# Expert products with two 64-column stationary halves in the main tiles, and one eviction per main tile

## What is computed

```
all_h   = einsum('bsd,ndr->bsnr', x, neurons)          # f_know: 128 matrices of 192 x 128
h       = einsum('bsnr,bsn->bsr', all_h, weights)      # only 4 weights per token are not zero
all_out = einsum('bsr,nrd->bsnd', h, neurons)          # r_know: 128 matrices of 128 x 192
out     = einsum('bsnd,bsn->bsd', all_out, weights)    # only 4 weights per token are not zero
```

## Time and profile before

| | us |
|---|---|
| median of 3 runs | 1011.28 |
| lowest and highest run | 1009.06 and 1013.69 |
| span of the profiled execution | 1005.3 |

### The profile page before, as it was taken

How to read it: one execution, slowest core, us unless ns; L and a number is a source line. 1 busy time by engine, 2 the same in 40 slices (tenths; PEclk the granted TensorE clock), 3 DMA queues, 4 the chain that set the end, 5 groups by cost and what they waited for, 6 DMA issues and landing times.

```text
span 1005.3 us, 21117 instructions
## 1 busy us (share of the span) xinstructions
PE 842.1 (84%) x5575; PEld 692.3 (69%) x5575; DVE 691.8 (69%) x4357; ACT 431.6 (43%) x1339; POOL 552.8 (55%) x764
## 2 busy tenths in 40 slices
PE   5789999999999999977731799999999799699900
PEld 3778888888888777754420688999988458565800
DVE  2199999999999899947694599874444244255423
ACT  0134334434444344425430254444544488578800
POOL 5256556665666565525477471007773677673065
PEclk9689989989999599967555799999999799899955
DMA  9233443443433265201732876557898677588533
GB/s 319 96 136 125 171 170 136 148 145 140 169 115 118 103 205 184 89 21 34 183 104 75 260 244 174 140 154 204 283 408 335 210 261 254 191 276 283 191 106 90
DMA packets 81580, 177.17 MB, mean 176 GB/s; under 512 B 12952, under 2 KB 38232, under 8 KB 78648
## 3 DMA queue, kind: packets, MB, share of 16 engines
q1 hardware_dynamic: 56088, 120.62, 37.2%
q10 hardware_dynamic: 14112, 32.12, 8.3%
q0 software_dynamic: 11264, 23.09, 7.7%
HBM read 94.25 MB, written 81.53 MB: 175 GB/s over the span
## 4 chain that ended last, share of the span: by engine, by line
PE 31%; DVE 28%; POOL 17%; issue 13%; ACT 6%; DMA 3%; SPq 1%; ACTq 1%; POOLq 0%; DVEq 0%
PE bank L1198 17%; DVE work L1335 12%; DVE top L1329 9%; ACT m_y L926 5%; POOL early L742 5%; PE bank L1186 4%; POOL slots_g L749 3%; POOL slots_x L720 3%; PE bank L1243 2%; PE bank L954 1%; PE bank L974 1%; POOL eqbd L622 1%; PE bank L999 1%; DMA early<-in_vocab,ids 1%; POOL sc L672 1%
## 5 line engine op out<-in xcount | busy, mean ns | idle before, releaser
L1335 DVE MATCH_REPLACE8 work<-top,work 128x68 f32<-128x68 f32 x896 | 179.2, 211 | 0.1
L906 ACT ACTIVATE m_y<-bank 64x128 f32<-64x128 f32 x392 | 106.3, 271 | 144.9 <-PE bank L1198 142.6
L926 ACT ACTIVATE m_y<-bank 64x192 f32<-64x192 f32 x392 | 127.1, 324 | 49.7 <-PE bank L1243 27.0
L1198 PE MATMUL bank<-f_all,place 96*128 (+1 forms) x792 | 146.3, 329 | 0.0
L1329 DVE MAX8 top<-work 128x8 f32<-128x68 f32 x896 | 128.9, 213 | 6.5 <-ACT tru L792 6.2
L1198 PEld LDWEIGHTS bank<-f_all,place 96*128 96x128 f32 x792 | 117.4, 193 | 7.4 <-issue 0.2
L1243 PE MATMUL bank<-r_all,place 128*128 (+1 forms) x396 | 118.2, 423 | 0.2 <-ACT m_y L926 0.2
L742 POOL DMA_INDIRECT early<-slots_h,s_all x68 | 65.6, 964 | 89.2 <-DMA slots_h<-m_y 68.8
L1604 DVE COPY place<-bank 96x256 f32<-96x256 f32 x147 | 57.4, 417 | 81.5 <-PE bank L1186 77.1
L1612 DVE COPY place<-bank 128x128 f32<-128x128 f32 x147 | 38.0, 287 | 100.8 <-PE bank L1234 100.6
L954 PE MATMUL bank<-early,xp 128*128 128x192 f32 x432 | 94.2, 382 | 6.7 <-DMA xp<-in_a_x 5.2
(11 more groups left out here) (187 smaller groups left out, 1692.9 us busy)
## 6 DMA issues: line engine op xcount, KB each, us to landing
early<-slots_x SPq DMA_DIRECT2D x49, 384.0 KB, 3.9
slots_y<-m_y ACTq DMA_DIRECT2D x49, 384.0 KB, 3.2
slots_h<-m_y ACTq DMA_DIRECT2D x49, 256.0 KB, 4.4
early<-slots_g SPq DMA_DIRECT2D x49, 256.0 KB, 3.3
f_all<-in_f_know SPq DMA_DIRECT2D x16, 768.0 KB, 9.3
r_all<-in_r_know SPq DMA_DIRECT2D x16, 768.0 KB
slots_x<-zero SPq DMA_DIRECT2D x28, 360.0 KB, 3.0
slots_x<-zero SPq DMA_DIRECT2D x28, 336.0 KB, 3.3
```

Source lines behind the costliest of these rows:

```text
L906: last = nc.scalar.activation(m_yh[rows, d, t, :], bank[2 + t][rows, h * R:(h + 1) * R], ACT.Copy)
L926: last = nc.scalar.activation(m_y[rows, d, t, :], bank[2 + t][rows, h * D:(h + 1) * D], ACT.Copy)
L1198: last = nc.tensor.matmul(into, m_xT[t][0:HALF, c, :], matrix[:, ..., c * R:(c + 1) * R], start=(c == 0), stop=(c == 1))
L1335: last = nc.vector.match_replace(work[:, par, c, :], top8[:, c, :], work[:, par, c, :], TAKEN)
```

## The change

In main tiles each expert's 64 token columns become a stationary operand of their own. Half `h` multiplies only its own matrix and writes its own 64 partitions of the bank, at the same columns for both halves. The order is: for each feature half `c`, expert 0 and then expert 1. A main tile of the first product is then eight passes of 128 columns in place of four of 256, and of the second four passes of 192 in place of two of 384. ACT evicts a main tile with one instruction over 128 partitions in place of two over 64. Spill tiles, transposes, copies, loads, stores and all semaphores stay as they are.

```diff
--- before.py
+++ after.py
@@ -901,9 +901,12 @@
                     act.wait_ge(sem[f"m_out{d}"], 16 * (j // DEPTH))
                 for t in range(GROUP):
                     act.wait_ge(sem["m_mm0"], j * GROUP + t + 1)
-                    for h in range(2):
-                        rows = slice(h * HALVED, (h + 1) * HALVED)
-                        last = nc.scalar.activation(m_yh[rows, d, t, :], bank[2 + t][rows, h * R:(h + 1) * R], ACT.Copy)
+                    if first_order(g)[n] < PART_MAIN:
+                        last = nc.scalar.activation(m_yh[:, d, t, :], bank[2 + t][:, 0:R], ACT.Copy)
+                    else:
+                        for h in range(2):
+                            rows = slice(h * HALVED, (h + 1) * HALVED)
+                            last = nc.scalar.activation(m_yh[rows, d, t, :], bank[2 + t][rows, h * R:(h + 1) * R], ACT.Copy)
                     last.then_inc(sem["m_done0"], 1)
                 act.wait_ge(sem["m_done0"], (j + 1) * GROUP)
                 at = first_order(g)[n] * GROUP * P
@@ -921,9 +924,12 @@
                     act.wait_ge(sem[f"m_out{d}"], 16 * (in_turn(d, GROUPS) + j // DEPTH))
                 for t in range(GROUP):
                     act.wait_ge(sem["m_mm1"], j * GROUP + t + 1)
-                    for h in range(2):
-                        rows = slice(h * HALVED, (h + 1) * HALVED)
-                        last = nc.scalar.activation(m_y[rows, d, t, :], bank[2 + t][rows, h * D:(h + 1) * D], ACT.Copy)
+                    if j - FIRST_GROUP[g] < PART_MAIN:
+                        last = nc.scalar.activation(m_y[:, d, t, :], bank[2 + t][:, 0:D], ACT.Copy)
+                    else:
+                        for h in range(2):
+                            rows = slice(h * HALVED, (h + 1) * HALVED)
+                            last = nc.scalar.activation(m_y[rows, d, t, :], bank[2 + t][rows, h * D:(h + 1) * D], ACT.Copy)
                     last.then_inc(sem["m_done1"], 1)
                 act.wait_ge(sem["m_done1"], (j + 1) * GROUP)
                 act.dma_start(slots_y[g][(j - FIRST_GROUP[g]) * GROUP * P:(j - FIRST_GROUP[g] + 1) * GROUP * P, :].rearrange("(p t) d -> p t d", p=P),
@@ -1186,19 +1192,25 @@
                     last = nc.tensor.transpose(turn_bank[t][0:HALF, c * P:(c + 1) * P], m_x[:, d, t, c:D:2], ident[:])
                 last.then_inc(sem["m_turn0"], 1)
 
-            def multiply_first(j, t, pair):
+            def multiply_first(j, t, pair, fixed):
 
                 pe.wait_ge(sem["m_xt0"], j * GROUP + t + 1)
                 if j >= 1:
                     pe.wait_ge(sem["m_done0"], (j - 1) * GROUP + t + 1)
-                n = R * (2 // len(pair))
-                for h, matrix in enumerate(pair):
-                    into = bank[2 + t][:, h * n:(h + 1) * n]
+                if fixed:
                     for c in range(2):
-                        last = nc.tensor.matmul(into, m_xT[t][0:HALF, c, :], matrix[:, ..., c * R:(c + 1) * R], start=(c == 0), stop=(c == 1))
+                        for h, matrix in enumerate(pair):
+                            rows = slice(h * HALVED, (h + 1) * HALVED)
+                            last = nc.tensor.matmul(bank[2 + t][rows, 0:R], m_xT[t][0:HALF, c, rows], matrix[:, c * R:(c + 1) * R],
+                                                    start=(c == 0), stop=(c == 1))
+                else:
+                    for h, matrix in enumerate(pair):
+                        for c in range(2):
+                            last = nc.tensor.matmul(bank[2 + t][:, h * R:(h + 1) * R], m_xT[t][0:HALF, c, :], matrix[:, c * R:(c + 1) * R],
+                                                    start=(c == 0), stop=(c == 1))
                 last.then_inc(sem["m_mm0"], 1)
 
-            def first_product(g, n, pairs):
+            def first_product(g, n, pairs, fixed):
                 j = FIRST_GROUP[g] + n
                 for t in range(0, GROUP, AHEAD):
                     for ahead in range(t + AHEAD, t + 2 * AHEAD):
@@ -1207,7 +1219,7 @@
                         elif n + 1 < PART_GROUPS[g]:
                             turn_first(j + 1, ahead - GROUP)
                     for now in range(t, t + AHEAD):
-                        multiply_first(j, now, pairs[now])
+                        multiply_first(j, now, pairs[now], fixed)
 
             pe.wait_ge(sem["tiles_known"], 1)
             pe.wait_ge(sem["f_in0"], 16 * LATE)
@@ -1219,11 +1231,11 @@
                         pe.wait_ge(sem["f_in1"], 16 * (CHUNKS - LATE))
                     if jj < PART_MAIN:
                         at = [(jj * GROUP + t) * 2 for t in range(GROUP)]
-                        pairs = [[f_all[0:HALF, e:e + 2, :]] for e in at]
+                        pairs = [[f_all[0:HALF, e + h, :] for h in range(2)] for e in at]
                     else:
                         e = matrix_numbers(mybir.EngineType.PE, 2 * g, jj)
                         pairs = [[f_all[0:HALF, bass.ds(e[2 * t + h], 1), :].squeeze(1) for h in range(2)] for t in range(GROUP)]
-                    first_product(g, n, pairs)
+                    first_product(g, n, pairs, jj < PART_MAIN)
 
             def turn_second(j, t):
                 d = j % DEPTH
@@ -1233,17 +1245,20 @@
                     pe.wait_ge(sem["m_xt1"], (j - 1) * GROUP + t + 1)
                 nc.tensor.transpose(turn_bank[t][:, 0:P], m_h[:, d, t, :], ident[:]).then_inc(sem["m_turn1"], 1)
 
-            def multiply_second(j, t, pair):
+            def multiply_second(j, t, pair, fixed):
 
                 pe.wait_ge(sem["m_xt1"], j * GROUP + t + 1)
                 if j >= 1:
                     pe.wait_ge(sem["m_done1"], (j - 1) * GROUP + t + 1)
-                n = D * (2 // len(pair))
                 for h, matrix in enumerate(pair):
-                    last = nc.tensor.matmul(bank[2 + t][:, h * n:(h + 1) * n], m_xT[t][:, 0, :], matrix, start=True, stop=True)
+                    rows = slice(h * HALVED, (h + 1) * HALVED)
+                    if fixed:
+                        last = nc.tensor.matmul(bank[2 + t][rows, 0:D], m_xT[t][:, 0, rows], matrix, start=True, stop=True)
+                    else:
+                        last = nc.tensor.matmul(bank[2 + t][:, h * D:(h + 1) * D], m_xT[t][:, 0, :], matrix, start=True, stop=True)
                 last.then_inc(sem["m_mm1"], 1)
 
-            def second_product(g, j, pairs):
+            def second_product(g, j, pairs, fixed):
                 stop = FIRST_GROUP[g] + PART_GROUPS[g]
                 for t in range(0, GROUP, AHEAD):
                     for ahead in range(t + AHEAD, t + 2 * AHEAD):
@@ -1252,7 +1267,7 @@
                         elif j + 1 < stop:
                             turn_second(j + 1, ahead - GROUP)
                     for now in range(t, t + AHEAD):
-                        multiply_second(j, now, pairs[now])
+                        multiply_second(j, now, pairs[now], fixed)
 
             pe.wait_ge(sem["m_done0"], GROUPS * GROUP)
             pe.wait_ge(sem["r_in"], 16 * (NE // CHUNK))
@@ -1262,11 +1277,11 @@
                 for jj in range(PART_GROUPS[g]):
                     if jj < PART_MAIN:
                         at = [(jj * GROUP + t) * 2 for t in range(GROUP)]
-                        pairs = [[r_all[:, e:e + 2, :].rearrange("p e d -> p (e d)")] for e in at]
+                        pairs = [[r_all[:, e + h, :] for h in range(2)] for e in at]
                     else:
                         e = matrix_numbers(mybir.EngineType.PE, 2 * g + 1, jj)
                         pairs = [[r_all[:, bass.ds(e[2 * t + h], 1), :].squeeze(1) for h in range(2)] for t in range(GROUP)]
-                    second_product(g, FIRST_GROUP[g] + jj, pairs)
+                    second_product(g, FIRST_GROUP[g] + jj, pairs, jj < PART_MAIN)
 
 
         @block.vector
```

## The result

The changed kernel takes **987.61 us** in the median against 1010.17 for the kernel before in the same job. One of its four runs took 2220.68 us, for a reason that is not known, and the ratio leaves it out. The ratio of the means is 0.9768, 95% interval 0.9738 to 0.9798. The kernel is 2.3% faster, inside the predicted range and 7.6 us above the predicted 980. The profiled execution took 985.86 us for a span of 984.0, so 1.9 us lie around the span. The 6.0 us that were put down to the time around the instructions, and stood in the sum, had compared one execution's span with the median of others; most of it was spread between runs.

A forecast was written before the change was run, and what follows sets the result against it. PE was always busy in the first product, with DVE, DMA or POOL close behind, and POOL's chain delayed the second. Gains 3 + 15 + 13 = 31 us from span 1005.3 gave span 974, median 980, range 967 to 1015.

The forecast's parts named there:

- Overlap: PE, main tiles: passes on different column halves run together, 0.073 us each in the first product, 0.081 in the second.
- The change of width: PE, between full-width transposes and halves: going in and coming back was priced at 0.06 us per half group.
- the cheap end: Price for two changes of width, 0.06 us per half group, from a 32-column pass between full ones.
- the dear end: Price for two changes of width, 0.38 us, from a load that waited 0.19; with it the median would be 984.
- DVE as the bound of part 0: First product, part 0: DVE becomes the bound, groups take 4.1 to 4.2 us, gain 3 us (2.2 to 5.5).
- The sums: Part 1's first product and both parts' sums: POOL waits less for DVE's sums, gain 15 us (4.4 to 22.9).
- the two-thirds guess: Of POOL's 22.9 us of waiting for sums, two thirds, 15 us, were taken as gain, since DMA may be late.
- The second product's part 1: 16 main groups fall from 3.05 to 2.3 us each; with the first group's cold start, gain 13 us (5 to 18).
- POOL's wait for `slots_y`: Sign in the second product of part 1: the wait for its stores falls from 31.89 us to below 20.
- C: Rival: passes do not overlap and changing width costs nothing; 1014 us, the same within 0.5%; chance 0.07.
- D: Rival: no overlap, and the array empties at each change between transposes and halves; 8 to 39 us slower, 1023; chance 0.16.
- B: Rival: halves overlap but DMA keeps the time; gain 15 us, so 996; chance 0.13.

The follow-up runs named there:

- one_side: Changed kernel, but both 64-column halves go to columns 0 to 63, one after the other, with two evictions and feature halves innermost; 1045.61 us, 1.0367 of the kernel before.
- wide_turns: Changed kernel, but in the second product the next group's four transposes stand together and turned tiles alternate between two places; 985.12 us, 0.9772 of the kernel before.
- second_only: Changed kernel with halves and single eviction in the second product alone, the first product as before; 0.9814 of the kernel before.
- slow_r: Changed kernel, but the loads of `r_all` are spaced wider in part 1 so that rows come first; 984.77 us, 0.9763 of the kernel before.

## Why the prediction was right, and where it was not

**Overlap: right, a pass undersized in speed.** The prediction took 0.073 us per pass as the least that a 64-column pass could cost, from a row with 68 columns. It takes 0.053. The lower bound was none: that row's passes had no neighbour on other columns, so that it showed a series. (All of them lie on the same columns; `one_side` builds such a series and has 0.107 us per pass.)

**The change of width: mis-sized, and the two errors cancel in one product only.** Taken was the cheap end, 0.06 us per half group; it is 0.34, two of 0.17, near the dear end of 0.38. In the first product 0.44 + 0.85 + 0.34 = 1.63 meets the predicted 1.67 by chance (0.020 × 16 = 0.32 too much for the passes, 0.28 too little for the changes). In the second, where the passes were priced rightly (0.80 − 0.17 = 0.63 for eight, 0.079 each against 0.081), 1.17 stands where 0.93 was forecast. `wide_turns` takes two of four changes away and gets 0.30 us back. The variant of the sum with the dear end, 984, was nearer than 980. The Trainium skill's rule that changing the tiling mode drains the engine (TensorEngine Tiling (Array Packing), Key Properties) agrees with the 0.17 us at each change; that a drain is what costs them, no run shows. The row of the 32-column pass was the wrong neighbour to choose. It is not shown what in that pass made its change cheap.

**DVE as the bound of part 0: right, its worth at the lower end.** Groups of 4.18 us, predicted 4.1 to 4.2, with 14 waits of PE for DVE's copies. The gain was put at 3 us (2.2 to 5.5). By length it is 1.1 to 2.0 in five of the six profiles with the halves in this form, and 5.2 in the first profile of the changed kernel. What the term left out is the clock: it priced PE's half group at full speed, and in those five profiles PE runs at 0.50 for the first 13 to 16 us (6 in the kernel before), where its half group of 2.94 us, and not DVE's 2.09, is the bound.

**The sums: mechanism right, 15 us was too much.** POOL's waits for sums fell by 12.1 us, not 15, and the two stages they lie in by 10.9 and 11.8 together. More than half of that comes from the second product's part 0 (6.4 to 6.7 us in the stage to part 0's outputs, `second_only` alone too) and 4.6 to 5.8 from the first product. What remained is DMA, as the term feared: loads of rows behind `r_all`, and PE at half clock after the wait. `slow_r` shows that another order of the loads gains nothing; the two-thirds guess should have been made from the bytes still to come before the second product.

**The second product's part 1: right.** 11.4 us against 13 (5 to 18), in both pairs of profiles. It needs the halves and the single eviction together, as ACT's 3.11 us per group had said; ACT's price of one eviction was right. What holds the stage now is mostly PE's step of 2.34 us, with turned tiles that come late behind DVE's output sums in places, and DMA right behind (1.01 in the window from 888).

**A sign that was badly chosen.** POOL's wait for `slots_y` was to fall below 20 us and is 29.0. The gathers of part 0's rows that stand ahead of it ended earlier as well, so that both ends of the wait moved. The gain shows in the stage, not in the wait.

**The rivals.** C and D fall with the passes 0.05 us apart. D's condition, a half group over 2.17 us, is what `one_side` builds: 2.51 and 37 us slower, inside D's 8 to 39 and far from its 12, since both changes cost near their dear end. B is partly true: the sums fell 3 to 4 us short where DMA is full, and DMA stands in the chain of the next step (`wide_turns`), but it did not keep the time of this one.

Sum by terms, predicted and measured in the two pairs of profiles: part 0 3, and 5.2 or 1.8; sums 15, and 10.9 or 11.8; second product 13, and 11.4 or 11.4; in all 31, and 27.5 or 25.

Splitting the spill tiles in the same way was not tried.

## What to carry to other kernels

Two stationary operands of half the width ran at the same time here when they lay on different columns; on the same columns the split made the kernel slower than before it (1.037 against 0.977), and every passage between full-width and half-width work cost 0.17 us, so count the passages, not only the passes. A faster product is worth its evictions: look at the engine that empties the banks in the same stage, since here the halves alone gave 0.994 and with one eviction per tile 0.977. Where DMA is as busy as here (0.97 to 1.03 up to the next stage's start), spacing its loads differently can move the wait and not the end.

## What the runs showed that was not expected

- A pass of 64 stationary columns takes 0.107 us alone, close to the 0.112 of a 128-column pass in a spill tile, and 0.053 in a pair. The columns moved are 128 in each.
- The sides need not alternate pass by pass: with the side changing half as often the half group was 1.69 us against 1.64.
- After the wait of 2.92 us in part 1, PE's granted clock was 0.50 from 751 to 760 and each half group took 2.94 us in place of 1.64. Three of them are 3.9 us, more than the wait itself. After the wait of 2.41 us before, the clock was back at 1.00 within some 4 us.
- After the same wait of 19 to 20 us the granted clock reached 1.00 later in six of seven profiles with halves on two sides in the first product (13 to 20 us after the start) than in those without them (6 us), and part 0's gain shrank with it.
